# New instruction orders and PSUM places for five engines of an attention and mixture-of-experts block

## The reference

```python
q3 = (x @ wq).reshape(b, t, h, 3).transpose(0, 2, 1, 3)
k3 = (x @ wk).reshape(b, t, h, 3).transpose(0, 2, 1, 3)
dot_scores = jnp.einsum('bhtd,bhsd->bhts', q3, k3) * scale
geo_bias = q_on_dir[..., :, None] * k_on_dir[..., None, :]
attn = jax.nn.softmax(jnp.where(causal, dot_scores + geo_bias, -jnp.inf), axis=-1)
...
shared = new_gelu(xf @ Wfc_s + bfc_s) @ Wproj_s + bproj_s
topk_p, topk_i = jax.lax.top_k(probs, TOP_K)
for e in range(N_EXPERTS):
    h = new_gelu(xf @ Wfc[e] + bfc[e]) @ Wproj[e] + bproj[e]
    routed = routed + h * gate[:, e:e + 1]
```

## Time and profile before

| what | value |
|---|---|
| time, median of 3 runs | 649.78 us (647.6 to 656.1) |
| span of the profiled execution | 693.1 us |
| mean granted TensorE clock in it | 0.956 of full speed |
| busy PE, DVE, ACT, POOL | 577.4, 444.3, 423.6, 324.1 us |
| chain that ended last | PE 38%, DVE 25%, ACT 16%, issue 9%, another core or an unknown queue 6% |

### The profile page before, as it was taken

The page is one execution under the profiler, slowest core; times in us unless marked ns, Lnnn a source line. Parts: engine busy times, 40 slices in busy tenths (PEclk is TensorE's granted clock), DMA queues, the critical chain, the costliest instruction groups (busy, mean ns, idle before and its releaser), DMA issues.

```text
span 693.1 us, 15803 instructions
## 1 busy us (share of the span) xinstructions
PE 577.4 (83%) x5284; PEld 433.5 (63%) x5318; DVE 444.3 (64%) x1179; ACT 423.6 (61%) x711; POOL 324.1 (47%) x434
## 2 busy tenths in 40 slices
PE   2678898999899799898897899999897787478686
PEld 2455464665465466565485778787776575377686
DVE  7799977699995966789844534555431245264386
ACT  4355776375666686396594599989998153134231
POOL 6817256475854657486445011122513576431440
PEclk9899998999999999999999899999999799599899
DMA  6182630063733010011526476857767287277661
GB/s 168 32 296 87 193 122 5 27 183 92 204 122 95 13 29 20 16 32 50 208 63 205 146 223 200 256 177 240 240 204 232 82 259 232 72 210 268 195 194 52
DMA packets 62429, 99.48 MB, mean 144 GB/s; under 512 B 9020, under 2 KB 47840, under 8 KB 61920
## 3 DMA queue, kind: packets, MB, share of 16 engines
q1 hardware_dynamic: 58512, 90.62, 43.1%
q0 software_dynamic: 3840, 7.87, 3.6%
HBM read 83.37 MB, written 31.80 MB: 166 GB/s over the span
## 4 chain that ended last, share of the span: by engine, by line
PE 38%; DVE 25%; ACT 16%; issue 9%; another core or an unknown queue 6%; POOL 3%; DMA 2%; SPq 0%; POOLq 0%; DVEq 0%; ACTq 0%
DVE negmax L1063 11%; PE banks L1425 7%; PE banks L1504 6%; PE banks L1512 5%; ACT hblk L961 5%; PE banks L1335 4%; ACT probs L923 4%; PE banks L1384 4%; ACT L961 3%; PE banks L1487 2%; PE banks L1386 2%; DVE probs L1208 2%; ACT L923 2%; PE banks L1482 2%
## 5 line engine op out<-in xcount | busy, mean ns | idle before, releaser
L1063 DVE TENSOR_REDUCE negmax<-banks 128x2 f32<-128x1024 f32 (+3 forms) x192 | 192.2, 1038 | 40.1 <-PE banks L1386 32.1
L923 ACT ACTIVATE probs<-banks 128x1024 f32<-128x1024 f32 x160 | 156.0, 1025 | 31.8 <-PE banks L1406 19.8
L792 POOL TENSOR_SCALAR_AFFINE_SELECT probs<-probs 128x512 f32<-128x512 f32 x128 | 79.6, 640 | 183.4 <-ACT probs L923 182.7
L961 ACT ACTIVATE hblk<-banks,wcur 128x128 f32<-128x128 f32 x340 | 95.3, 376 | 99.2 <-PE banks L1504 53.5
L1504 PE MATMUL banks<-xblkT,wcur 128*128 128x128 f32 x680 | 99.7, 291 | 25.2 <-ACT hblk L961 10.9
L1384 PE MATMUL banks<-kpad,qst 128*128 128x384 bf16 (+3 forms) x478 | 107.2, 296 | 15.6 <-DVE negmax L1063 9.1
L1504 PEld LDWEIGHTS banks<-xblkT,wcur 128*128 128x128 f32 x680 | 88.8, 202 | 32.1 <-ACT hblk L961 13.4
L1512 PE MATMUL banks<-wcur,hblk 128*128 128x128 f32 x680 | 93.2, 281 | 10.6 <-ACT hblk L961 4.2
L1386 PE MATMUL banks<-future,identb 128*128 128x128 bf16 x512 | 96.4, 220 | 5.3 <-ACT probs L923 1.9
L1512 PEld LDWEIGHTS banks<-wcur,hblk 128*128 128x128 f32 x680 | 83.9, 194 | 17.0 <-issue 6.2
L830 POOL DMA_INDIRECT got<-ys,from_row x56 | 55.1, 984 | 68.3 <-issue 30.2
(11 more groups left out here) (157 smaller groups left out, 862.0 us busy)
## 6 DMA issues: line engine op xcount, KB each, us to landing
wcur<-wtab SPq DMA_DIRECT2D x85, 578.0 KB
xs<-in_L_attn_x SPq DMA_DIRECT2D x8, 1188.0 KB, 8.7
xblk<-xs SPq DMA_DIRECT2D x85, 64.0 KB
ys<-yblk SPq DMA_DIRECT2D x34, 128.0 KB
kpad<-kst SPq DMA_DIRECT2D x64, 64.0 KB, 3.0
xs<-in_L_attn_x SPq DMA_DIRECT2D x8, 505.0 KB
acc<-in_L_attn_x SPq DMA_DIRECT2D x8, 256.0 KB, 5.1
wtab<-in_L_ffn_Wfc SPq DMA_DIRECT2D x2, 1024.0 KB
```

Of the source, the lines that this page charges most:

```text
L792: pool.affine_select(out=v, in_=v, compare_op=ALU.is_ge, fill=0.0, base=0, pattern=[[0, R], [1, P]], channel_multiplier=-1).then_inc(maske ...
L923: nc.scalar.activation(probs[:, g % 2, heads[0]:heads[-1] + 1, at:at + P * sum(EUNITS[unit])], src, ACT.Exp).then_inc(exp_done, 1)
L961: ins = nc.scalar.activation(hblk[:, k % 3, q, :], one(PLACE["HB", g, s])[:, P * q:P * q + P], ACT.Gelu_apprx_tanh, bias=wcur[:, k % NW, 2 ...
L1063: dve.tensor_reduce(negmax[:, g, tiles - 1, heads[0]:heads[-1] + 1], unit_view(PLACE["M", b, n], tiles), AX.X, ALU.max, negate=True).then_ ...
```

## The change

All five tables are replaced. Each of the new ones holds exactly the steps of the old one in another order (781 on TensorE, 393 on ScalarE, 492 on VectorE, 234 on GpSimd, 228 on SyncE), and the TensorE steps have other PSUM places; the small units now use banks 0 to 7 where before they used mostly 4 to 7. No function is changed. The line numbers behind the tables are 8 lower. The new tables were planned with the pairs of indirect transfers of SC and GA held apart. The first lines of two tables:

```diff
 TENSOR_ORDER = """
-    T1.0.0@6 QKV.0.1@6 QKV.0.0@7 BT.0.0@5 T1.1.0@6 TQ.0.0@6 TK.0.0@7 TK.0.1@5 TQ.0.1@6 QKV.1.1@7 QKV.1.0@6
+    T1.0.0@7 BT.0.0@6 QKV.0.0@7 QKV.0.1@6 T1.1.0@7 TK.0.0@6 TK.0.1@7 QKV.1.0@5 QKV.1.1@4 TQ.0.0@6 M.0.6@0
...
 VECTOR_ORDER = """
-    S1.1.0 QK.0.1 BE.0.0 QK.0.0 S1.2.0 SK.0.0 S1.3.0 QK.1.1 QK.1.0 MX.0.4 MX.0.0 MX.0.1 MX.0.2 MX.0.3 MX.0.5
+    BE.0.0 S1.1.0 QK.0.0 QK.0.1 SK.0.0 S1.2.0 QK.1.0 QK.1.1 S1.3.0 MX.0.6 MX.0.4 MX.0.7 MX.0.0 MX.0.1 MX.0.5
...
-    YE.2.3 SB.2.8 CB.6.0 XV.2.6 SB.2.9 YE.2.4 CB.6.1 XV.2.7 SB.2.10 SB.2.11 SB.2.12 YE.2.5 SB.2.13 YE.2.6
-    SB.2.14 YE.2.7 CB.7.0 CB.7.1
+    CB.5.1 XV.2.7 YE.2.5 SB.2.11 SB.2.12 SB.2.13 YE.2.6 SB.2.14 YE.2.7 CB.6.0 CB.7.0 CB.7.1 CB.6.1
```

More of the change, by code:

```diff
@@ new lines @@
+    TK.5.1@5 T2.3.0@4 M.5.0@2 M.4.21@0 M.5.2@6 H.3.0@4 E.4.8@2 H.3.2@5 RL.3.0@1 TM.4.3@0 PV.4.1@3 H.3.3@2
+    H.3.1@5 E.4.10@60 M.5.10@2 Y.3.0@5 RK.3.0@4 Y.3.1@5 M.5.4@2 E.4.11@0 QKV.6.1@4 M.5.7@6 E.4.9@2 Y.3.2@5
+    E.4.7@6 Y.3.3@5 M.5.3@2 M.5.17@4 M.5.6@6 TP.4.1@5 M.5.12@0 PV.4.3@3 M.5.8@4 PV.4.2@2 TM.5.0@3 M.5.9@0
+    M.5.13@4 E.5.0@62 QKV.6.0@1 TP.4.2@0 E.5.1@42 TM.5.1@7 TP.4.3@6 M.5.15@2 M.5.16@0 TO.4.0@6 T1.7.0@7 M.5.18@4
+    E.5.5@2 PJ.4.0@6 E.5.2@0 M.5.23@5 E.5.4@62 M.5.14@0 M.5.22@2 TK.6.0@5 E.5.3@60 QKV.7.1@4 M.5.19@2 TQ.6.0@7
@@ new lines @@
+    E.6.6@40 M.7.18@6 Y.5.0@2 XT.0.8@3 Y.5.1@2 YB.0.12@3 E.6.9@64 E.6.11@0 YB.0.13@3 HB.0.14@7 HB.0.15@6
+    HB.0.17@3 XT.0.9@5 HB.0.16@4 M.7.19@0 YB.0.14@7 XT.0.10@5 YB.0.15@7 YB.0.16@6 E.6.10@40 Y.5.2@2 HB.0.18@7
+    YB.0.17@6 HB.0.19@3 XT.0.11@6 Y.5.3@2 M.7.22@0 HB.0.20@5 M.7.23@7 HB.0.21@4 YB.0.18@6 TP.6.1@7 YB.0.19@6
+    E.6.8@0 E.6.7@42 PV.6.3@7 HB.0.22@6 YB.0.20@1 XT.0.13@0 YB.0.21@1 M.7.0@2 HB.0.23@7 XT.0.12@1 M.7.20@4
+    M.7.3@2 YB.0.22@6 M.7.2@0 YB.0.23@6 M.7.7@2 HB.0.24@7 M.7.1@4 PV.6.2@6 HB.0.25@7 HB.0.27@6 TM.7.0@5
@@ new lines @@
+    YB.0.24@4 XT.0.14@7 M.7.21@0 TP.6.2@3 HB.0.26@7 YB.0.25@4 HB.0.28@5 E.7.0@20 TP.6.3@7 YB.0.26@6 XT.0.15@4
+    YB.0.27@6 E.7.2@4 M.7.17@7 TO.6.0@6 HB.0.29@3 M.7.8@0 YB.0.28@2 HB.0.30@5 M.7.10@0 HB.0.31@7 YB.0.29@2
+    PJ.6.0@6 XT.0.16@5 M.7.6@0 YB.0.30@7 HB.0.32@6 HB.0.33@5 YB.0.31@7 XT.0.17@6 E.7.1@20 M.7.9@4 HB.0.34@7
+    M.7.13@4 YB.0.32@6 M.7.16@0 T2.6.0@5 YB.0.33@6 XT.0.18@7 TM.7.1@4 RL.6.0@5 HB.0.35@7 E.7.3@40 HB.0.36@6
+    HB.0.37@3 H.6.3@2 YB.0.34@1 PV.7.0@0 YB.0.35@1 H.6.2@7 E.7.5@0 RK.6.0@6 YB.0.36@3 XT.0.19@2 YB.0.37@3
@@ L137 @@
+    YB.2.14@6 CM.2.11@4 YB.2.13@7 CM.2.12@4 CM.2.13@4 CM.2.14@4
 """
 SCALAR_ORDER = """
[L140 to L143 removed]
@@ new lines @@
+    KE.2.0 OE.0.1 EX.0.13 EX.0.12 EX.0.19 EX.0.11 EX.0.10 KE.2.1 QE.2.0 OE.0.2 EX.0.15 EX.0.16 EX.0.18 EX.0.17
+    EX.1.0 EX.1.1 EX.1.4 OE.0.3 EX.1.2 EX.1.3 HE.0.0 EX.1.6 EX.1.5 OE.1.0 EX.1.9 EX.1.14 EX.1.7 EX.1.8 VS.3.0
+    EX.1.11 VS.3.1 EX.1.10 QE.2.1 X2.0.0 EX.1.13 EX.1.12 OE.1.1 LX.0.0 GS.0.2 GS.0.0 GS.0.1 GS.0.3 OE.1.2
+    EX.1.15 EX.1.16 EX.1.19 EX.1.17 EX.1.18 KE.3.0 OE.1.3 QE.3.0 HE.1.0 EX.2.0 XE.4.0 EX.2.1 EX.2.4 QE.3.1
+    EX.2.9 KE.3.1 EX.2.2 EX.2.3 VS.4.0 X2.1.0 LX.1.0 GS.1.2 VS.4.1 GS.1.3 GS.1.1 GS.1.0 EX.2.5 EX.2.6 EX.2.8
@@ new lines @@
+    SC.0.3 VX.3.0 N2.2.0 MK.3.3 MK.3.1 MK.3.2 MK.3.0 N1.6.0 BS.2.0 MK.3.4 SC.1.3 MK.3.5 MK.3.7 MK.3.6 SC.1.2
+    MK.3.9 MK.3.8 MK.3.11 MK.3.10 SC.2.2 MK.3.14 SQ.5.0 SK.5.0 MK.3.12 MK.3.13 MK.3.15 MK.4.0 SC.1.0 MK.4.2
+    MK.4.1 MK.4.3 VX.4.0 SC.2.3 N2.3.0 MK.4.6 MK.4.7 MK.4.5 MK.4.4 SC.2.0 MK.4.8 SC.2.1 MK.4.10 BS.3.0 SC.3.0
+    MK.4.14 MK.4.15 MK.4.13 MK.4.12 SC.3.2 MK.4.11 MK.4.9 N1.7.0 SK.6.0 MK.5.0 VX.5.0 SQ.6.0 N2.4.0 MK.5.3
+    MK.5.2 SC.3.3 MK.5.4 MK.5.1 SC.3.1 BS.4.0 MK.5.6 MK.5.7 MK.5.5 SC.4.1 SK.7.0 SC.4.0 SQ.7.0 SC.4.2 MK.5.8
@@ L248 @@
+    YS.1.7 WC.2.0 YS.1.8 XB.2.0 WC.2.1 YS.1.9 XB.2.1 OU.2.1 XB.2.2 WC.2.2 WC.2.3 WC.2.4 XB.2.3 WC.2.5 WC.2.6
+    YS.1.10 YS.1.11 WC.2.7 OU.3.1 XB.2.4 WC.2.8 WC.2.9 XB.2.5 OU.2.0 WC.2.10 OU.4.0 WC.2.11 XB.2.6 OU.0.0
+    WC.2.12 XB.2.7 OU.0.1 WC.2.13 OU.1.1 OU.3.0 OU.5.0 WC.2.14 OU.4.1 OU.5.1 OU.7.0 OU.7.1 OU.6.0 OU.6.1
 """
```

290 lines of the change are left out of this document (127 added, 163 removed).

## The result

The changed kernel takes 626.6 us (median of four runs, 620.98 to 628.15) against 650.38 us of the kernel before in the same comparison: ratio 0.9641, 95% interval 0.9573 to 0.9708. That is 23.8 us or 3.6% faster. The forecast was 643.0 us with a range of 621 to 656: the direction and the range held, the size was too small by 16.4 us.

What follows compares the result with a forecast made beforehand. It took TensorE, nearly full beside a full ScalarE from 400 to 480 us, as the limit. Terms 0 - 7.0 - 1.2 + 0 + 1.4 = -6.8 us took 649.78 to 643.0 us; own range 634 to 652, stated range 621 to 656.

Steps and rivals of the forecast that it cites:

- the two fast rivals: Transfer stalls also in timed runs (628 us), or ScalarE's saved table loads gained in full (622 us); chance 0.13 each.
- Reading of the profile: The 693.1 us span exceeds timed runs because waits at bunched GpSimd transfers belong to the profiled execution.
- the five pieces of 39.5 us: Chain waits on "another core or an unknown queue", where GpSimd issues indirect transfers one behind the other.
- Pairs held apart: GpSimd's indirect transfers spaced by masks: 0 in timed runs, up to 14.8 us saved in the profile.
- Table loads: ScalarE loses 24 of 60 exp/gelu loads, 30.8 us; 70% of TensorE's 10.0 us idle time taken: -7.0 us.
- The rival that paid them in full: ScalarE's relief from fewer table loads is on the path in full, 28.2 us: 622 us, chance 0.13.
- Start: Third batch's statistics moved behind the key spread on VectorE, keys turned first: -1.2 us, between -2.5 and 0.
- Attention: From 30 to 270 us, maxima, scores and values change places: 0 taken, up to 10 us either way.
- the sentence that would have made the prediction wrong: The prediction is wrong if time changes mainly in attention, to which it gave nothing.
- End: Last VectorE step becomes batch 6's combine, two stores follow batch 7's: +1.4 us, between 0 and +2.3.
- The slower rival: Longer exp runs on ScalarE delay gelus and starve TensorE's second products: 665 to 674 us, chance 0.12.
- Stalls in the timed runs: Rival: bunched transfers stall timed runs too, so spacing pairs saves another 14.8 us: 628 us, chance 0.13.

Runs made afterwards that it cites:

- run 1: The kernel before, unchanged, timed and profiled again: ratio 1.0021, ten runs of 645.96 to 656.34 us.
- run 4: The kernel before with exp in place of gelu, so that all table loads but the first go: ratio 0.9863, 643.27 us.
- run 5: The changed kernel with exp in place of gelu, so that its 36 table loads but the first go: ratio 0.9635 to the kernel before, 625.22 us.
- run 6: The kernel before with combines later on VectorE, behind evacuations TensorE waits for, and stores late on SyncE: ratio 0.9996, 649.39 us.
- run 7: The kernel before with late combines and late stores, and batch 3's row numbers also later on VectorE: ratio 1.0087, 653.91 us.
- run 2: The kernel before with GpSimd's order alone changed, pairs of indirect transfers held apart by masks: ratio 1.0041, 654.0 us.

## Why the prediction was right or wrong

The measured 626.6 us lies in the stated range, but outside the forecast's own 634 to 652 us. The range held because it took in the two fast rivals, and the runs refute the mechanisms of both: that is luck. The own range doesn't quite come out of the ends that it names, which give 635 to 650 us, and it leaves out the bounds of the loads, 0 to 28.2 us.

- **Reading of the profile: right.** That the five pieces of 39.5 us were the profiled execution's own is shown by run 1. The cause I gave, transfers bunched behind each other, isn't: the same bunches stand in run 1 without a piece. (The matmuls in the earlier trace rows follow each other by 1.4 us, not by the 1.3 of the transfers.) The rule I weighed there, from the Trainium skill, page "NOTIFIC — the notification-queue block", section "7.1 Overflow: three behaviours, one of which stalls the engine", would put such a stall into the recording; thirteen recorded executions without one neither show nor refute it.
- **Pairs held apart, 0: right.** +0.4% in the kernel before, at most some 4 us in the changed one, and there the first gather comes earlier too.
- **Table loads, -7.0: right as far as the runs can tell.** 5.4 to 8.5 us by runs 4 and 5, open by some 5.6 us. The rival that paid them in full comes near the measured time with its 622 us, but by a cause that runs 4 and 5 exclude: all 59 loads together were worth 7 to 9 us.
- **Start, -1.2: the step is there, its worth isn't settled.** SyncE issues kpad from 21.92 us on instead of 22.98, but the eight issues end at 30.42 instead of 28.26, and the first maximum starts only 0.2 us earlier. The first two residuals are 2.8 and 0.7 us earlier, so it doesn't simply carry on.
- **Attention, 0: perhaps mis-sized.** The residual of the last batch comes 3.7 us earlier, inside the bounds of 10 us. One execution of each doesn't settle that: with one and the same order of attention the residual of batch 1 starts at 134.89 us in run 6, 135.78 in run 1 and 139.73 in run 7. It isn't the main part, so the sentence that would have made the prediction wrong doesn't apply.
- **End, +1.4: this step failed.** Its own small piece came as worked out: CB.6.1 now ends last, 1.2 us behind the last batch's combine.

```profile
621.69 0.76 DVE L1210 TENSOR_TENSOR acc<-banks,acc 128x256 f32<-128x256 f32 x2
...
622.36 1.25 DVE L1252 SCALAR_TENSOR_TENSOR acc<-got,wtop,acc 128x128 f32<-128x128 f32 x4
```

  But I looked at the last instructions only, and took what lies between attention and them for unchanged. The sum has no term for the first gathers, the routing of the last batch and the blocks behind, and gives no reason. That stretch gave 16 of the 19.6 us: 8.8 between the mean and TensorE's transposes and 9.6 behind the row numbers; the 0.5 and the 2.9 of the table, with their signs, take 2.4 off again. The first gather starts 15.4 us earlier, and with it fall both the norm's wait and TensorE's waits for VectorE. GpSimd's order stood in front of me with N2.7 behind nine pairs of gathers, and VectorE's with blocks' rows behind combines; I read them for pairs of transfers, not for who waits behind them.
- **The slower rival: refuted.** TensorE's second products wait 0.4 us for hblk in the whole changed kernel, 2.2 us before. The rival also priced all 11 runs of exps at five; in the new table only two of them have five or more.
- **Stalls in the timed runs:** its 628 us is the nearest number of all, and its mechanism is out by runs 1 and 2. A number that fits is no evidence for its story.
- **What I said the profile would show:** 36 loads, yes (687 ACT instructions against 652 in run 5, which keeps one); ScalarE down by 10 us from 400 to 480 us, by 21.8; TensorE about 78 of 80, 76.55; a span near 671, no, since 693.1 was no base.

## What to carry to other kernels

Where a queue serves two chains (here GpSimd: gathers of finished work and the norm of the last batch), look at what stands behind each waiting step, and on which chain that is, before pricing the step itself. Then look at the engine for which the result is meant: if it comes later still, the wait is worth nothing by itself, and two waits side by side have to go together. A full engine beside a full engine isn't the bound; take its load away in a run before believing it, and take it away from both kernels: the difference of the two gives what it was worth in the change. And profile a kernel twice before building on a wait that only one profile shows.
